# Layer-0 attention: the row mask added by VectorE in the instruction that takes the maximum, in place of mask products on TensorE

## What is computed

```python
causal = k_pos[None, :] <= q_pos[:, None]
in_window = k_pos[None, :] >= q_pos[:, None] - WINDOW + 1
meta = k_pos[None, :] < meta_end
allowed = causal & (in_window | meta)
scores = jnp.einsum('bhqd,bhkd->bhqk', q_c, k_c) * scale
scores = jnp.where(allowed[None, None], scores, -jnp.inf)
attn = jax.nn.softmax(scores, axis=-1)
```

## Time and profile before

| | us |
|---|---|
| median of 3 runs | 1409.88 (1407.91 to 1418.24) |
| the profiled execution: its own time | 1409.83 |
| the profiled execution: span from first to last instruction | 1408.0 |
| PE matmul busy | 1277.4 (91%) |
| DVE busy | 670.7 (48%) |
| ACT busy | 526.5 (37%) |
| POOL busy | 692.5 (49%) |

### The profile page before, as it was taken

The page is one execution under the profiler, slowest core; times in us unless marked ns, Lnnn a source line. Parts: engine busy times, 40 slices in busy tenths (PEclk is TensorE's granted clock), DMA queues, the critical chain, the costliest instruction groups (busy, mean ns, idle before and its releaser), DMA issues. The chain is left out here.

```text
span 1408.0 us, 20445 instructions
## 1 busy us (share of the span) xinstructions
PE 1277.4 (91%) x7267; PEld 1033.1 (73%) x7267; DVE 670.7 (48%) x1362; ACT 526.5 (37%) x1135; POOL 692.5 (49%) x552
## 2 busy tenths in 40 slices
PE   4488899999952899999999999999999986999998
PEld 4366588888842788788888888888888873666655
DVE  4698655565527356755464435433443331222223
ACT  2354466665534433333433334333433321011110
POOL 3343476676635356577576665665565550000014
PEclk9789999999985899999999999999999997999999
DMA  6700277777744322121212111111111107411113
GB/s 218 273 1 1 55 162 155 156 159 155 167 106 146 109 65 66 33 75 61 76 60 72 35 60 65 50 49 60 35 49 46 35 0 288 164 47 48 46 57 115
DMA packets 97988, 127.39 MB, mean 90 GB/s; under 512 B 11744, under 2 KB 81248, under 8 KB 97760
## 3 DMA queue, kind: packets, MB, share of 16 engines
q1 hardware_dynamic: 82912, 99.85, 22.1%
q0 software_dynamic: 14976, 26.23, 9.4%
HBM read 97.83 MB, written 28.21 MB: 90 GB/s over the span
## 5 line engine op out<-in xcount | busy, mean ns | idle before, releaser
L1430 PE MATMUL a_p_p<-a_xr,a_wr 128*128 128x512 f32 x1152 | 309.5, 404 | 2.4 <-DVE g_x L1991 2.4
L1430 PEld LDWEIGHTS a_p_p<-a_xr,a_wr 128*128 128x128 f32 x1152 | 207.2, 189 | 42.8 <-DVE g_x L1991 3.1
L1763 POOL TENSOR_TENSOR a_sqsum<-a_sqsum,a_sq 128x512 f32<-128x512 f32 x60 | 78.0, 1300 | 228.1 <-ACT a_sq L1623 228.1
L1716 POOL TENSOR_TENSOR a_wr<-a_w,a_wr 128x768 fp32r<-128x768 f32 x64 | 123.7, 1933 | 20.2 <-DVE a_wr L1791 20.2
L365 POOL DMA_INDIRECT acc<-l_ye,g_slot_token x64 | 102.1, 1595 | 61.3 <-ACT l_ye L695 47.4
L1825 DVE SCALAR_TENSOR_TENSOR a_gated<-a_th,a_p_o 128x512 f32<-128x512 f32 x64 | 44.0, 688 | 159.2 <-ACT a_sq L1623 159.2
L1442 PE MATMUL a_p_p<-a_wvr,a_xr 128*128 128x512 f32 x384 | 107.6, 418 | 3.0 <-POOL a_xr L1712 3.0
L1765 POOL TENSOR_TENSOR a_gr<-a_gated,a_gr 128x512 fp32r<-128x512 f32 x64 | 97.7, 1526 | 23.7 <-DVE a_gr L1829 23.7
L1044 POOL DMA_DIRECT2D out<-e_ye x24 | 13.1, 546 | 193.6 <-DVE e_ye L1194 193.6
L1498 PE MATMUL a_p_w<-a_gr,l_wo_r 128*128 128x512 f32 x384 | 100.1, 395 | 2.3 <-POOL a_gr L1765 2.3
L1480 PE MATMUL a_p_o<-a_sc,a_v 128*128 128x128 f32 x512 | 89.6, 277 | 5.4 <-DVE a_sc L1805 5.4
(11 more groups left out here) (249 smaller groups left out, 2763.0 us busy)
## 6 DMA issues: line engine op xcount, KB each, us to landing
a_w<-in_Wqkg SPq DMA_DIRECT2D x64, 384.0 KB, 3.2
l_up<-in_gate_up SPq DMA_DIRECT2D x64, 192.0 KB, 2.8
a_wv<-in_Wv SPq DMA_DIRECT2D x16, 512.0 KB, 4.4
e_up<-in_gate_up SPq DMA_DIRECT2D x8, 1024.0 KB, 13.6
l_down<-in_down SPq DMA_DIRECT2D x64, 96.0 KB, 3.1
acc<-l_zero SPq DMA_DIRECT2D x2, 2176.0 KB, 11.5
e_down<-in_down SPq DMA_DIRECT2D x8, 512.0 KB, 12.3
rows<-l_zero SPq DMA_DIRECT2D x1, 3072.0 KB, 21.0
```

The source lines that it names most:

```text
L1430: mm = pe.matmul(dst[:, :], wr[n % 2][:, wp, kk, c * P:(c + 1) * P], xr[n // H1 % 2][:, xp, kk, :], start=(kk, xp, wp) == (0, 0, 0), stop= ...
L1716: pool.tensor_tensor(wr[n % 2][:, 1, :, :], w[n % 2][:, :, :], wr[n % 2][:, 0, :, :], ALU.subtract).then_inc(w_parts, 1)
L1763: pool.tensor_tensor(sqsum[b % 2][:, :], sqsum[b % 2][:, :], sq[a % 2][:, :], ALU.add).then_inc(summed, 1)
```

## The change

The mask product (L461) is gone, and the first score product of each head now starts its part of the bank. On VectorE the one reduction for a bank is replaced by two `tensor_tensor_reduce`, one to a head: each adds the mask to the 208 scores of a head, writes the sum to a bf16 tile that nobody reads, and takes the maximum into one column of `top`. The first of each bank waits on one semaphore more (`max_done`, for the reuse of the bf16 tiles, or `rounded` in step 0, for the mask). The mask tile is no longer written twice. The scores with keys down the partitions (`turn_scores`) and their mask products stay as they are.

```diff
-        mask = m.sb("mask", [P, 2, 2, KEYS0], BF16)
+        mask = m.sb("mask", [P, 2, KEYS0], BF16)
+        masked = [m.sb(f"masked{s}", [P, KEYS0], BF16) for s in range(4)]
...
-            pool.tensor_copy(mask[:, :, :, :], maskf[:, :, :].unsqueeze(2).to_broadcast([P, 2, 2, KEYS0])).then_inc(rounded, 1)
+            pool.tensor_copy(mask[:, :, :], maskf[:, :, :]).then_inc(rounded, 1)
...
                     bank = p_s[pp % 2]
-                    pe.matmul(bank[:, :, 0:KEYS0], identb[:, :], mask[:, kind(t), :, :], start=True, stop=False,
-                              skip_group_check=True)
                     for i in range(2):
                         mm = pe.matmul(bank[:, i, 0:KEYS0], qT[t % 3][:, kv // 2, 2 * c + i, :], kz[:, kv, t % TPB, :],
-                                       start=False, stop=True, skip_group_check=True)
+                                       start=True, stop=True, skip_group_check=True)
                     mm.then_inc(scored, 1)
...
                     dve.wait_ge(scored, pp + 1)
-                    dve.tensor_reduce(top[n % 3][:, 2 * c:2 * c + 2], p_s[pp % 2][:, :, 0:KEYS0], AX_X, ALU.max).then_inc(max_done, 1)
+                    if n == 0:
+                        dve.wait_ge(rounded, ROUNDED)
+                    else:
+                        dve.wait_ge(max_done, pp - 1)
+                    for i in range(2):
+                        at = 2 * c + i
+                        ins = dve.tensor_tensor_reduce(masked[at][:, :], p_s[pp % 2][:, i, 0:KEYS0], mask[:, kind(n // G0), :], 1.0, 2.0 * MASKED,
+                                                       ALU.add, ALU.max, top[n % 3][:, at:at + 1])
+                    ins.then_inc(max_done, 1)
```

## The result

| | us |
|---|---|
| before, median of 20 runs | 1410.09 (1407.39 to 1418.33) |
| after, median of 20 runs | 1418.28 (1412.49 to 1425.73) |
| after / before | 1.005, 95% interval 1.0032 to 1.0068 |
| the profiled executions: span before, after | 1408.0, 1419.3 |
| DVE busy before, after | 670.7, 685.2 |

The kernel is slower by 0.5%, about 8 us: 4 us less than forecast, inside the range, and not beyond the 1% that I gave as the border. Three of my terms were wrong all the same, and they cancelled.

What follows compares the result with a forecast made beforehand. VectorE was taken to bound the first half of layer 0's attention, TensorE the second. Changes of +10.2 and +2.0 us made +12.1 on the profiled 1409.83 us: forecast 1422 us, range 1406 to 1440.

Steps and rivals of the forecast that it cites:

- The pass: VectorE's new reduction over 208 columns, four a step: 0.29 us from start to start, 0.37 us long.
- The small write: VectorE's write of a maximum after each pass, four a step, priced at 0.12 us each.
- x: What a step's maxima on VectorE take beyond the 1.12 us before the change; taken as 0.63 us.
- my lower bound: Step's maxima on VectorE if the small write costs nothing: 1.27 us, so x = 0.15.
- First half: Layer 0's attention, steps 0 to 21, VectorE deciding: 19.5x - 2.1, +10.2 us to the first gather.
- TensorE's saving: Mask products dropped: 0.35 us a step, counted only where TensorE decides; 11.5 us in the sum at x = 0.
- after it the next step keeps 0.25 and the last 0.35: Second-half rounds of four steps: TensorE's saving kept after its wait for `hT`, 0.6 us a round.
- a wait for `hT`: Second half: TensorE waits for `hT` behind VectorE's maxima, some 1.9 us a round, swallowing its saving in two steps.
- Second half: Layer 0's attention, steps 22 to 63, TensorE deciding: 18x - 9.4, +2.0 us at x = 0.63.
- The sum: Both halves of layer 0's attention together: 37.5x - 11.5, +12.1 us.
- The rival of cheap small writes: VectorE's small writes overlap the next pass, x under 0.45: 1404 us at x = 0.15, 1415 at 0.45; chance 0.2.
- Wrong if the slot list comes under 4 us later: Refuting sign at the first half's end: VectorE's slot list under 4 us later, x then under 0.3.

Runs made afterwards that it cites:

- e1: The kernel after with short memsets on GpSimd that start its long operations later, so that `diag` comes ahead of them; ratio to before 0.9996.
- e4: The kernel before without the mask products on TensorE, its old maxima taken over unmasked scores (TensorE's part alone); ratio to before 0.9974.
- e12: The kernel after with e1's GpSimd memsets, e6's ScalarE order, and e11's VectorE order and six `ye` buffers; ratio to before 0.9985.
- e11: e6 with the rotation of tiles 8 to 15 behind a step's maxima and first silu on VectorE, and six `ye` buffers; ratio to before 0.9911.
- e8: The kernel after, unchanged, run and profiled again on the same chip as e7; ratio to before 1.0049.
- e6: e4 with ScalarE's copy of `ye` moved ahead of its copies of V and of the keys' spread, from step 24 on; ratio to before 0.9956.
- e2: The kernel before with a 160-column VectorE memset ahead of `diag` in steps 0 to 21; ratio to before 1.0006.
- e3: The kernel after with TensorE's mask products put back, the mask added twice (VectorE's part alone); ratio to before 1.006.
- e7: The kernel before, unchanged, run and profiled again on the same chip as e8; ratio to before 1.0001.

## Why the prediction was right or wrong

**The pass: right. The small write: wrong, and it is the step that failed first.** I had 0.29 us from pass to pass and 0.37 of length; measured are 0.29 and 0.367. I took 0.12 us for each small write, "midway". It is 0.08 us long and costs 0, since the next pass starts with it. So x is 0.17, next to my lower bound of 0.15, where I had taken 0.63. (The column price in that sum, 1.05 ns, should read 1.09 by its two rows; it changes none of these figures by 0.01 us.) The nearest neighbour said so: the four small results of the earlier trace rows followed each other in 0.08 us, and the second of the two products there began before the first had ended. The rule of the Trainium skill that I had weighed ("VectorE: DVE Perf Modes", "The DRAIN you can't avoid") would have made x 0.71. The trace disagrees with it as I applied it, at the full length for each pass; the same section adds that an operation that is not held starts earlier, which I had left out.

**First half: 10.2 us forecast, 9.3 and 6.5 measured, for another reason.** At x = 0.17 my sum gives 19.5 x 0.17 - 2.1 = 1.2 us, and e1, the kernel without the long `diag`s, has 0.7. The total fits, but its two terms do not. The 2.1 us of TensorE's saving were not there: e4, at x = 0, has a first half that is 0.5 us longer, because the wait in step 21 grew by 1.3 us at a lower clock, where I had counted 0.35 won. The maxima cost less than the 3.3 us of 19.5 x 0.17 as well: e12 against e11 has 2.2, and e1 against e4 only 0.1. What the sum lacked altogether is the 5.9 us (5.4 in e8) that GpSimd takes from `diag`. I treated `diag` as an instruction that is only moved. With both inputs in SBUF and a GpSimd product of two SBUF tensors 0.16 us behind it, its start was worth looking at. The Trainium skill, "SBUF — State Buffer", section "Who interferes with whom", has the rule that I didn't apply: a VectorE instruction with two SBUF inputs and a GpSimd instruction that reads SBUF exclude each other, and the one that issued first holds the other for its whole length. The trace agrees, with 0.88 us of product and then 0.27 of `diag`, and with the mirror case in e1. There the hold is somewhat shorter than the recorded length: the product lasts 0.19 us more than alone, while `diag` still had 0.33 us to run (84.18 to 84.51).

**TensorE's saving: 11.5 us forecast at x = 0, 3.7 measured (e4).** In the second half the step that failed is "after it the next step keeps 0.25 and the last 0.35". In e4 the next one keeps 0.50 and the last loses 0.28. I checked for each `expert_out` how early its `hT` was, and for nothing else. At the transposes of the next rows TensorE had no visible wait before, but no reserve either: the copy of `ye` was done just as its turn came. The mechanism that I had named, a wait for `hT`, is real, but it is second in line, as e6 shows. In after the wait before L535 is 0.7 us in all and not 1.9 a round; the gaps stand before L552.

**Second half: +2.0 us forecast, -2.2 and -2.7 measured.** With x = 0.17 the formula gives 18 x 0.17 - 9.4 = -6.3. I put the missing 4 us down to the saving that wasn't kept. The profiles of one chip bear that out only in part, with 4 to 6 us kept of the 9.4 (e4 against e2, whose second half is before's: 235.4 and 241.6; e1 against e3: 237.4 and 241.6), and the profiled executions of e1 and e4 were the fastest of their runs.

**The weight of x: not settled.** My 37.5 x 0.17 is 6.4 us. Up to the last `diag`, e12 against e11 has 2.2 + 2.8 = 5.0 by the profiles, and e1 against e4 has 0.1 + 2.0 = 2.1. By the ratios the same pairs differ by 10.5 and by 3.1 us. In the second half of e3 the passes cost nothing (241.6 us in e2 and in e3), where my formula has 18 x 0.17 = 3.1. So the formula has the right order of size, but a step's 0.17 us are not worth the same in these kernels, and why is open.

**The sum.** 37.5 x 0.17 - 11.5 = -5.1; the collision adds 5.9; the saving that TensorE doesn't keep adds 11.5 - 3.7 = 7.8. Together +8.6 us, against 8.2 on the first chip and 6.7 on that of e7 and e8, by the medians. That this comes so near is in part chance, since the parts do not simply add: VectorE's part alone (e3) and TensorE's alone (e4) give 8.5 - 3.7 = 4.8 us, and after is 7 us over before by its ratio. My +12.1 came near it by luck: a write priced 0.12 us too dear stood in for the terms that I had not seen. The rival of cheap small writes had the right x and the wrong sum (1404 us).

**What was to show it.** Passes of 0.37 us: yes. Small ones near 0.1: 0.081. From the first pass to `diag` 1.75 us: 1.29. The slot list at 168: 165.74. Rounds that keep their length within half a microsecond: yes, 22.35 against 22.57. TensorE waiting for `hT` some 1.9 us a round: no, 0.7 us in all. The last scores 12 us later: 5.4. A granted clock that falls in the second half: from 200 us on it was 1.00 before and after; from the slot list to 200 us it was 0.96 before and 0.90 after, and 0.92 and 0.85 in e7 and e8, so that this sign was there in part. "Wrong if the slot list comes under 4 us later (x then under 0.3)": it came 8 us later with x at 0.17, so the sign that I had chosen could not tell x from a collision. The length from the first pass to `diag` could.

## What to carry to other kernels

An instruction that reads two SBUF tensors on VectorE can have a price that depends on 0.1 us (here 0.42 or 0.91 to 1.16 us for `diag`): list what GpSimd starts within its length before and after any change that moves it, and if it must be near, put the engine that isn't on the path second. A gapless engine keeps a saving only as far as every input that it takes next was early; read the reserve of each releaser at each of its waits, ScalarE's copies that free a PSUM bank included, before counting the saving. Take the parts apart, and check that they add up, even where the whole comes out as forecast. And when a price lies between two bounds, take the one of the nearest kind of instruction, not the middle.

## What the runs showed of the hardware

- The accumulator's write-out behind a `tensor_tensor_reduce` of 208 columns lasts 0.075 to 0.085 us (256 of them) and overlaps with the next pass: a step's four passes, of 0.367 us each, follow each other in 0.29 us.
- `diag` (0.42 us alone) lasts 0.91 to 1.16 us when a GpSimd `tensor_tensor` starts up to 0.1 us ahead of it or together with it; it then ends 0.28 us behind that operation, in all 12 cases. The operation, where it is the product of 320 columns, lasts 1.05 instead of 0.87 when `diag` is first. Three fillers of 0.18 us together on GpSimd turned the one into the other.
- A VectorE memset of 256 columns that runs when GpSimd's product of 320 columns starts, with `diag` right behind it, makes the product last 1.19 us; where the product started 0.06 us ahead of a memset of 160 columns, the product lasted 0.87 and `diag` 0.98 (one case).
- TensorE's granted clock in step 21 was 0.54 in one profile of after and 1.00 in another, and VectorE's wait there was 3.61 us in the first and 1.60 in the second. In e4 it was 2.87 us at 0.72, against 1.58 at 1.00 in before.
